# A macaron block on one core: value products over all 128 rows against a zero-padded p, with p's transposition copied in two halves

## The reference

```python
def local_attention(q, k, v):            # b, h, n, d = 2, 16, 1024, 64
    bq = q.reshape(b, h, nw, w, d)       # w = 32, nw = 32
    ...
    bk2, bv2 = (look(bk), look(bv))      # each window with the one before it: 64 keys
    ...
    sim = jnp.einsum('bhwie,bhwje->bhwij', bq, bk2) * QK_SCALE
    sim = jnp.where(mask, -jnp.finfo(sim.dtype).max, sim)
    attn = jax.nn.softmax(sim, -1)
    out = jnp.einsum('bhwij,bhwje->bhwie', attn, bv2)
```

## Time and profile before

| | |
|---|---|
| median of three runs | 3309.44 us |
| the profiled execution: time | 3317.88 us |
| the profiled execution: span of the core | 3316.0 us |
| TensorE matmuls (PE) | 96% of the span |
| TensorE weight loads (PEld) | 72% |
| VectorE | 83% |
| ScalarE | 77% |
| GpSimd | 67% |
| TensorE clock granted | 0.995 of full |

### The profile page before, as it was taken

The page is one execution under the profiler, slowest core; times in us unless marked ns, Lnnn a source line. Parts: engine busy times, 40 slices in busy tenths (PEclk is TensorE's granted clock), DMA queues, the critical chain, the costliest instruction groups (busy, mean ns, idle before and its releaser), DMA issues. The chain is left out here.

```text
span 3316.0 us, 150147 instructions
## 1 busy us (share of the span) xinstructions
PE 3177.3 (96%) x63272; PEld 2384.7 (72%) x63464; DVE 2748.5 (83%) x6951; ACT 2545.5 (77%) x4144; POOL 2226.4 (67%) x1453
## 2 busy tenths in 40 slices
PE   7999999999999999999999999999999999999997
PEld 4777777777777777777777777777777777777776
DVE  7888888888888888889998888888888888888885
ACT  3777777777777777777777777777777777777775
POOL 6666666666666666667887666666666666666663
PEclk9999999999999999999999999999999999999999
DMA  4111111111111111111111111111111111111111
GB/s 124 45 48 45 48 44 48 45 48 45 47 42 43 48 45 48 45 48 45 47 39 45 48 44 48 45 46 41 45 48 45 48 44 48 45 44 43 47 52 38
DMA packets 135089, 157.39 MB, mean 47 GB/s; under 512 B 75539, under 2 KB 108439, under 8 KB 134423
## 3 DMA queue, kind: packets, MB, share of 16 engines
q1 hardware_dynamic: 129815, 144.42, 15.7%
q10 hardware_dynamic: 4608, 3.34, 0.3%
HBM read 33.38 MB, written 1.05 MB: 10 GB/s over the span
## 5 line engine op out<-in xcount | busy, mean ns | idle before, releaser
L1073 POOL TENSOR_TENSOR rot<-rot,swp 128x1024 f32<-128x1024 f32 x384 | 907.0, 2362 | 137.8 <-DVE rot L866 137.8
L482 PE MATMUL proj<-wq,xsT 128*128 128x512 f32 x1536 | 769.6, 622 | 27.6 <-DVE rot L866 10.3
L673 ACT ACTIVATE sq<-proj 128x512 f32<-128x512 f32 x768 | 438.0, 596 | 416.1 <-PE proj L482 406.3
L1082 POOL TENSOR_TENSOR rot<-rot,rn 128x1024 f32<-128x1024 f32 x384 | 724.4, 1908 | 0.0
L1063 POOL TENSOR_TENSOR rt<-rt,half 128x1 f32<-128x1 f32 x192 | 105.3, 549 | 755.6 <-DVE rt L936 755.6
L860 DVE TENSOR_TENSOR swp<-proj,tab 128x512 f32<-128x512 f32 x768 | 521.3, 679 | 12.2 <-ACT sq L673 7.2
L866 DVE TENSOR_TENSOR rot<-proj,tab 128x512 f32<-128x512 f32 x768 | 517.9, 674 | 0.8 <-PE tps L493 0.8
L990 DVE SCALAR_TENSOR_TENSOR hT<-proj,cols,fg 114x128 f32<-114x128 f32 (+1 forms) x576 | 166.7, 345 | 417.7 <-ACT fg L739 413.6
L493 PEld LDWEIGHTS tps<-idf,rot 128*128 128x128 f32 x3072 | 360.2, 141 | 206.2 <-issue 204.1
L1067 POOL TENSOR_TENSOR prob<-prob,rr 128x1024 f32<-128x1024 f32 x192 | 365.4, 1903 | 174.9 <-DVE rr L948 174.9
L482 PEld LDWEIGHTS proj<-wq,xsT 128*128 128x128 f32 x1536 | 259.8, 190 | 254.9 <-issue 145.4
(11 more groups left out here) (102 smaller groups left out, 5873.0 us busy)
## 6 DMA issues: line engine op xcount, KB each, us to landing
vb<-va SPq DMA_DIRECT2D x192, 384.0 KB, 3.5
vb<-va SPq DMA_DIRECT2D x192, 128.0 KB, 3.6
wq<-in_L_ffn_Wqkv SPq DMA_DIRECT2D x95, 192.0 KB, 3.4
xs<-Z SPq DMA_DIRECT2D x192, 32.0 KB
wo<-in_L_ffn_Wo SPq DMA_DIRECT2D x94, 64.0 KB, 2.8
xs<-Z SPq DMA_DIRECT2D x192, 28.0 KB
xs<-Z SPq DMA_DIRECT2D x192, 3.8 KB
xs<-Z SPq DMA_DIRECT2D x192, 0.2 KB
```

What stands on the lines that cost most here:

```text
L482: mm(proj[:, c % 2, :], xsT[:, k.parity(L_QKV), 0:P], wq2[:, bass.ds(w + c * 512, 512)], start=True, stop=True).then_inc(p_qkv[c], 1)
L673: fn(sq[:, c * 512:(c + 1) * 512], proj[:, c % 2, :], ACT.Square).then_inc(a_sq[c], 1)
L1073: g_.tensor_tensor(r, r, swp[:, g * INNER:(g + 1) * INNER], ALU.add).then_inc(g_add[g], 1)
L1082: g_.tensor_tensor(r, r, rn[:, g * HEADS:(g + 1) * HEADS].unsqueeze(2) .to_broadcast([P, HEADS, DH]), ALU.mult).then_inc(g_nm[g], 1)
```

## The change

The tile `pT` grows from 8 x 128 to 16 x 2 x 2 x 32 columns (16 pairs of head pair and g, then hp, t and the position i in the window), and is zeroed once by GpSimd. ScalarE writes the rows of half t only into the columns of the same t, so the block of the other t stays zero. A product over all 128 rows then gives the windows of both t in 64 columns at once. The values are a 128 x 64 load in place of two of 64 x 64.

```diff
-        pT = sb("pT", [PAIRS, P])
+        pT = sb("pT", [PAIRS * 2, 2, 2, WIN])
...
             def attend(k):
                 par = k.parity(L_AV)
                 for p in range(PAIRS):
+                    o4 = ops[:, p // 4, (p % 4) * P:(p % 4 + 1) * P].rearrange("p (t g i) -> p t g i", t=2, g=2)
                     for g in range(2):
                         for hp in range(2):
-                            for t in range(2):
-                                o4 = ops[:, t, p * 64:(p + 1) * 64].rearrange("p (g i) -> p g i", g=2)
-                                at = (2 * p + hp) * DH
-                                rows = slice(t * DH, (t + 1) * DH)
-                                v = vb[rows, at:at + DH] if g == 0 else va[rows, par, at:at + DH]
-                                to = (2 * g + (hp ^ t)) * WIN
-                                last = mm(o4[hp * DH:(hp + 1) * DH, g, :], v, pT[rows, p, to:to + WIN],
-                                          start=True, stop=True, skip_group_check=True)
+                            at = (2 * p + hp) * DH
+                            v = vb[:, at:at + DH] if g == 0 else va[:, par, at:at + DH]
+                            last = mm(o4[hp * DH:(hp + 1) * DH, :, g, :], v,
+                                      pT[:, 2 * p + g, hp, :, :].rearrange("p t i -> p (t i)"),
+                                      start=True, stop=True, skip_group_check=True)
...
-                    cp(oT[:, :, :].rearrange("p a (t x) -> p t a x", t=2),
-                       ops[:, :, :].rearrange("p t (a x) -> p t a x", x=2 * WIN)).then_inc(a_oT, 1)
+                    cp(oT[:, :, :], ops[:, :, :].rearrange("p b (a x) -> p (b a) x", x=P)).then_inc(a_oT, 1)
...
-                    cp(pT[:, :, :], tps[:, :, :]).then_inc(a_pT, 1)
+                    if k.s == L_SM:
+                        act.wait_ge(c_pz, 1)
+                    for t in range(2):
+                        rows = slice(t * DH, (t + 1) * DH)
+                        src = tps[rows, :, :]
+                        swapped = bass.AP(src.tensor, src.offset + t * WIN,
+                                          [list(src.ap[0]), [2 * WIN, 2 * PAIRS], [(1 - 2 * t) * WIN, 2], [1, WIN]])
+                        last = cp(pT[rows, :, :, t, :], swapped)
+                    last.then_inc(a_pT, 1)
...
+                if s == 0:
+                    g_.memset(pT[:, :, :, :, :], 0.0).then_inc(c_pz, 1)
```

More of the change, by code:

```diff
@@ L141, in macaron @@
         c_zero, c_zero2 = sem("c_zero"), sem("c_zero2")
+        c_pz = sem("c_pz")
         s_idb, s_mask = sem("s_idb"), sem("s_mask")
```

## The result

| | before | after |
|---|---|---|
| median | 3308.28 us (4 runs, 3306.02 to 3310.67) | 3354.15 us (4 runs, 3352.26 to 3356.53) |
| the profiled execution: time, span | 3317.88, 3316.0 us | 3354.89, 3353.1 us |
| TensorE clock granted | 0.995 | 0.997 |

The changed kernel is slower: ratio 1.014, 95% interval [1.0128, 1.0152]. The forecast was 3357.

A forecast was written before the change was run, and what follows sets the result against it. TensorE, busy 96%, was taken to bound the kernel, with ScalarE holding its next projection by 0.18 us. Terms 0 - 10 + 58 + 0 = +48 us took the median from 3309.44 to 3357; range 3316 to 3400.

The forecast's parts named there:

- ScalarE's second copy: On ScalarE, copying p in halves adds a whole copy of 1.02 us, delaying TensorE's next projection and scores: +58 us.
- second copy 596.47, xnT 597.38: Predicted ScalarE start times in a step: p's second half copy, then xnT, overlapping it by 0.1 us.
- The value products: On TensorE, 32 pairs per column half at 59 ns take 1.88 us, the same as before: 0 us.
- rival B: In the value products, loads no longer overlap with matmuls: slower, +1.8 us a step, +346, 3700 us; 7%.
- rival A: In the value products, instruction count and not array time decides, 64 pairs take 0.94 us: faster, 3177 us; 4%.
- Instruction supply: On TensorE, halving the value products' loads and matmuls removes their 12 waits for instructions: -10 us.
- The holes in the scores stay: TensorE's 68 unexplained waits inside the scores, 71.4 us in all, were to remain, a packet boundary still falling there each step.
- rival C: With 128 fewer instructions a step, the scores' 68 holes vanish too: faster by 85 us, 3272 us; 8%.
- the small terms: Zeroing on GpSimd, 2.2 us once, hidden behind a wait, and a slightly shorter copy to oT: 0 us, or +2 uncovered.
- D: ScalarE's added copy falls within its idle 1.09 us, or both effects cancel: 3309 - 10 to 3309 + 6; 6%.

The follow-up runs named there:

- experiment 1: The kernel before with p's transposition copied in two halves of 64 partitions, the old value products kept: 3390.16 us, ratio 1.0231.
- experiment 9: The kernel before with p's copy in two instructions, each of 128 rows and 512 columns: 3311.3 us, ratio 1.0.
- experiment 3: The changed kernel with the second half copy of p moved to the head of ScalarE's next step: 3278.67 us, ratio 0.9899.
- experiment 2: The changed kernel with only the first of its two half copies of p, all new products still running: 3278.98 us, ratio 0.9894.
- experiment 4: The kernel of experiment 3 with the 64 old value products of 64 rows and the old `pT`: 3313.02 us, ratio 1.0013.
- experiment 6: The kernel of experiment 3 with 64 more TensorE instructions per step that only wait for a semaphore long past: 3465.98 us.
- experiments 5 and 6: The kernel of experiment 3 with added TensorE instructions that only wait for a past semaphore: 128 per step 4794.98 us, 64 per step 3465.98 us.

## Why the prediction came out right

The sign and the engine that decides it were foreseen; that the time is so close, 3354 for 3357, is luck. Two terms of the sum were each some 20 to 25 us too small by the medians (30 and 39 by the blocks of the profiled executions), with opposite signs.

**ScalarE's second copy: the mechanism was right, the size too small.** The forecast term was +58; experiment 1 measured the copy in halves by itself at +77. As forecast, the second copy is a whole one (2.02 us for two, in experiment 9 1.07 for two of half the columns), it uses up both pauses, L502 waits for `va`, and the wait goes when the second half moves away (experiment 3). The part that was mis-sized is "second copy 596.47, xnT 597.38": I let xnT overlap the second half's end by 0.1 us, as it overlaps the full copy in the earlier trace rows, though I had denied the overlap to the pair L746 and L747. After the upper half, which covers 64 partitions, xnT over 128 partitions waits: 2.05 us after the start in place of 1.93. Those 0.12 us move all behind: measured from the start of p's copy, the mask comes 0.56 later than before where I had 0.41 (4.71 against 4.15), and L483 0.40 later where I had 0.24 (6.45 against 6.05). 0.12 x 192 = 23 us, and 58 + 23 = 81, near the 77; the whole 0.16 by which L483 misses would make 89, near the 88 of the blocks. L483 is now held by the scores and no longer by `xsT`.

**The value products: right.** 32 x 59 ns was the forecast, with a gain of at most 0.10 us a step and a loss of 0.03. The median block went from 1.998 to 2.015 us, 3 us in all. Had a load no longer overlapped with the matmuls (rival B), it would have shown as +1.8 us a step. The durations of the new loads and matmuls, as the earlier trace rows has the old ones, the kernel after:

```profile
L538 PEld LDWEIGHTS ops<-pT,vb x6144: 132/138/138, 64.8 to 3334.5; 128*64 128x64 f32 x199
L538 PE MATMUL ops<-pT,vb x6144: 222/222/271, 64.8 to 3334.6; 128*64 128x64 f32 x199
```

Each load now covers all rows of the array, and 64 pairs of 138 and 222 ns still fit into 2.015 us. The rule that I had set against this, in the Trainium skill, page "TensorE: Matmul & The Clock Gate", section "Part 3: Packing small matmuls — row/col tiling", that a load overlaps with matmuls in flight only when its row group is another, does not hold in this trace. One figure of rival A was wrong: it would decide from a gain of 0.25 us over 32 pairs, 8 ns each, so from a pair of 51 ns and not of 44. At the measured 2.015 us nothing hangs on it.

**Instruction supply: the step that was wrong.** "The holes in the scores stay" failed, and rival C, to which I gave 8%, came true for about two fifths: its 85 us became 38.8 + 45 x 0.2 = 48. The forecast term was -10, the value products' own holes, and these did go (12 to none). But the scores' holes went from 68 to 45, and in experiments 2 and 4 the whole term is -34. My argument was that the scores and the 100 instructions ahead of them are the same, so a packet boundary still falls in them once a step. It does: counting TensorE's instruction stream in packets of 256 (some 130,300 instructions before, for 509 packets), each of the 192 groups of scores has one, spread evenly, before and after. The count also bears out that the holes are waits for a packet: all 68 of before and all 45 of after stand at the same place of it, two neighbouring instructions (number 193 or 194 of 0 to 255 by this count), and so do those of every other kernel here. That place is called the boundary here.

What changed is how often the packet behind it is late. Of the boundaries that lie at instruction 160 to 191 of the scores, 23 of 25 had a hole before and 5 of 25 after; from 192 on it is 44 of 49 and 40 of 50. Where the boundary lies at 170 to 178, the latest fetch had begun 0.98 to 1.15 us ahead of the scores in eight of nine such steps of before (0.46 in the ninth), and the scores stood still until 1.5 to 1.75 us after their start; in the changed kernel it had begun 2.7 to 7.3 us ahead in all eight, and none had a hole. The other kernels agree. Of the 25 or so boundaries at 160 to 191 the latest fetch had begun 1.3 to 10 us ahead of the scores in 1 before, none in experiment 1, 4 in experiment 4 and 2 in experiment 9, all with the old products; in 19 after, 17 in experiment 2 and 18 in experiment 3; and in all 25 of experiment 6, which has the fewest holes. Not one of these had a hole.

That the fetch starts earlier is seen. Why it does is not: the boundary ahead of it was passed 5.7 to 6.2 us ahead of the scores before and 6.3 to 6.8 after, so TensorE's own use of the stream does not show it, the number of instructions in a step does not decide it alone (experiments 5 and 6), and no run here varied what stands where in a packet by itself. It stays open.

**Of the small terms,** the memset and the copy to `oT` show in no wait. Together: +77 - 34 = +43 for +46 measured; forecast +58 - 10 = +48. Of the rivals, A (products bound by issue, 3177), B and D fell.

Of what was to be seen, the products' 2.0 us, the missing pauses and the vanished holes in the products were there. The mask 0.4 later was 0.56, the step of 16.66 us was 16.80 to 16.91, and the "about 68" holes were 45.

## What to carry to other kernels

A term whose sign is clear can still hide another of the opposite sign. Run each half of a change by itself before a slower total is taken as the worth of both. Here the half that had looked worthless, fewer and larger products, is worth 34 us, and the half that came with it needed only another place: at the head of the next step, where ScalarE waits anyway, its copy costs nothing. If a ScalarE copy must be split, split its columns; if rows must be split, look on that engine for idle time a step later, and count a full copy for each part.

## What the runs showed of the hardware

- A ScalarE copy from PSUM takes its time by columns: 64 x 1,024 took 1.01 us, as long as 128 x 1,024; two of 128 x 512 took 1.07.
- Neighbouring ScalarE instructions of 128 partitions overlap by 0.1 us where the later one waits for nothing and no table is loaded between them. A copy of the upper 64 partitions overlapped neither the lower half ahead of it (2.02 for two) nor the 128-partition xnT behind it (0.03 between them), but one of the lower 64 did (experiment 3: L683 at 608.68 lasts 1.01, L735 starts at 609.59). Behind another instruction of the upper 64 the upper copy overlaps as well (experiment 3: L758 at 614.38 lasts 0.20, L683 starts at 614.49).
- A load and a matmul over twice the rows and twice the moving columns cost what two such pairs in quadrants cost: 64 pairs in 2.015 us, 128 pairs in 1.998.
- TensorE can stand up to 2 us for its next instruction when 256 small loads and matmuls pass in 1.5 us (longest 1.8 before, 2.0 in experiment 9). All these holes fall at one place of a packet of 256 instructions (68 of 68 before, 45 of 45 after).
- An instruction that only waits for a semaphore long past is not free on TensorE's queue: 15 ns each with 64 a step, 62 ns with 128 (at a granted clock of 0.94).
